# Picks between the maxima, norms transposed inside the up-embedding product, half of the row comparison on GpSimd, keys in two row halves

## The reference

```python
# attention: 16 heads of 16; keys and values from a 64-wide context, causal
qp = layernorm(x) @ Wq.T ; k, v = split(ctx @ Wkv_expand.T)
x = x + tanh(g_xattn) * (softmax(causal(q k^T / 4)) v) @ Wout.T
# experts: 2048, 8 heads, 45 keys for each of two halves of the query
h = silu(layernorm(x) @ W_up.T + b_up) @ W_down.T + b_down
sx, ix = top_k(q0 keys0, 8); sy, iy = top_k(q1 keys1, 8)
sc, pk = top_k(all 64 sums sx + sy, 8); indices = chosen ix * 45 + iy
z = silu((h . down_embed[indices]) * softmax(sc))
x = x + tanh(g_ffn) * sum over (head, k) of z * up_embed[indices]
```

## Time and profile before

| | us |
|---|---|
| median of 3 runs | 1230.05 (1229.36 to 1233.81) |
| profiled execution, its own time | 1228.0 |
| its span | 1226.3 |
| mean granted TensorE clock | 0.983 |

### The profile page before, as it was taken

One profiled execution on the slowest core, in us unless ns is written; L12 is line 12 of the kernel. 1 busy time (PEld: TensorE's weight loads), 2 busy tenths in 40 slices (PEclk: granted clock), 3 DMA queues, 4 the chain that ended last, 5 costly groups with the idle time before them and its releaser, 6 DMA issues. The chain is left out here.

```text
span 1226.3 us, 47601 instructions
## 1 busy us (share of the span) xinstructions
PE 1151.3 (94%) x19004; PEld 1029.6 (84%) x19004; DVE 1071.6 (87%) x4298; ACT 702.8 (57%) x2474; POOL 330.4 (27%) x149
## 2 busy tenths in 40 slices
PE   6778999999999999999999999999999999999957
PEld 4567888888888888888888888889888888988856
DVE  3359999999999999999999999999999999998983
ACT  4565555566655656665555666656566665656310
POOL 4022333212333331223333122333312233331210
PEclk9988999999999999999999999999999999999979
DMA  8015556445645654465565446556544655654454
GB/s 217 13 71 144 106 127 150 122 116 135 147 106 130 150 134 118 121 151 115 118 150 133 123 118 150 118 114 150 135 117 121 150 117 117 149 140 106 130 134 72
DMA packets 304948, 154.52 MB, mean 126 GB/s; under 512 B 282736, under 2 KB 295896, under 8 KB 296536
## 3 DMA queue, kind: packets, MB, share of 16 engines
q1 hardware_dynamic: 304727, 151.47, 51.2%
HBM read 79.62 MB, written 4.72 MB: 69 GB/s over the span
## 5 line engine op out<-in xcount | busy, mean ns | idle before, releaser
L354 POOL TENSOR_TENSOR rstd<-veps,minus_half 128x1 f32<-128x1 f32 x32 | 67.9, 2123 | 718.0 <-DVE veps L805 718.0
L1131 PE MATMUL bank<-ue,coef 128*128 128x256 f32 x1024 | 227.7, 381 | 0.7 <-ACT coef L413 0.7
L1131 PEld LDWEIGHTS bank<-ue,coef 128*128 128x128 f32 x1024 | 193.0, 191 | 25.9 <-ACT coef L413 0.8
L910 PEld LDWEIGHTS bank<-z,hot_rT 128*128 128x128 bf16 x2048 | 155.8, 96 | 42.5 <-issue 29.0
L910 PE MATMUL bank<-z,hot_rT 128*128 128x32 bf16 x2048 | 165.1, 177 | 18.0 <-DVE picked L618 12.6
L453 ACT ACTIVATE P<-bank,smax 128x64 f32<-128x64 f32 x512 | 151.8, 348 | 46.4 <-DVE smax L646 46.2
L927 PE MATMUL bank<-uc,hot_r 128*128 128x32 bf16 x6144 | 161.3, 176 | 13.1 <-issue 12.8
L927 PEld LDWEIGHTS bank<-uc,hot_r 128*128 128x128 bf16 x6144 | 158.1, 96 | 14.9 <-issue 14.2
L910 PE MATMUL bank<-zl,hot_rT 128*128 128x32 bf16 x2048 | 163.9, 177 | 3.6 <-issue 3.6
L910 PE MATMUL bank<-zll,hot_rT 128*128 128x32 bf16 x2048 | 163.9, 177 | 0.2 <-issue 0.2
L910 PEld LDWEIGHTS bank<-zl,hot_rT 128*128 128x128 bf16 x2048 | 156.6, 96 | 3.8 <-issue 3.7
(11 more groups left out here) (142 smaller groups left out, 2301.1 us busy)
## 6 DMA issues: line engine op xcount, KB each, us to landing
hot_rT<-expert_rows SPq DMA_DIRECT2D x64, 1024.0 KB, 6.5
xt<-in_x SPq DMA_DIRECT2D x32, 128.0 KB, 2.4
out<-x1k SPq DMA_DIRECT2D x32, 128.0 KB, 2.1
ct<-in_ctx SPq DMA_DIRECT2D x32, 64.0 KB, 2.1
ue<-in_L_ffn_up_embed SPq DMA_DIRECT2D x1, 2048.0 KB, 13.0
z<-in_L_ffn_W_up SPq DMA_DIRECT2D x1, 1024.0 KB, 8.3
expert_rows<-r_h SPq DMA_DIRECT2D x64, 8.0 KB, 1.8
hot_r<-hot_rT SPq DMA_TRANSPOSE x64, 7.0
```

The costliest lines, as they stand in the source:

```text
L354: nc.gpsimd.tensor_tensor(rstd[:, :], veps[:, :], minus_half[:, :], ALU.pow).then_inc(S["rstd_ok"], 1)
L910: last = mm(bank[:, 32 * (q - 16 * k):32 * (q - 16 * k) + 32], hot_rT[:, q, :], part.rearrange("r (h q) c -> r h q c", h=2)[:, :, q, :], s ...
L1131: last = mm(bG0[:, 0:DM], coef[:, c, :, :].rearrange("r h q -> r (h q)"), ue[:, c, :], start=(c == 0), stop=(c == C - 1))
```

## The change

TensorE puts the transposes of the second norm (`normed_T`) and of the next tile's first norm and context (`inputs_T`, before at the head of the next turn) between the twelfth and the thirteenth of the 16 output products. The second key product takes its operands from partitions 64 to 127 and writes another bank; `k_diag` is written by eight ScalarE instructions of half the size. VectorE does picks 0, maximum 0, picks 1, maximum 1, and the sums later. The second half of the comparison (`hot_T(1)`) is done by GpSimd, as the first thing in its turn.

```diff
 # gpsimd, head of the turn
+                if B:
+                    B.wait_dma("rows_in1")
+                    nc.gpsimd.tensor_scalar(hot_rT[:, Q // 2:Q, :], hot_rT[:, Q // 2:Q, :], p_iota[:, 0:1], None, ALU.is_equal).then_inc(S["hotrT1"], 1)
 # scalar
-                    for h in range(4):
-                        last = nc.scalar.activation(k_diag[:, :, :, h, :], bD[:, 256:512].rearrange("p (a b k) -> p a b k", a=2, b=2),
-                                                    ACT.Copy, scale=head_of[:, h:h + 1])
+                    for a in range(2):
+                        for h in range(4):
+                            last = nc.scalar.activation(k_diag[:, a, :, h, :], (bD, bT)[a][:, 384:512].rearrange("p (b k) -> p b k", b=2),
+                                                        ACT.Copy, scale=head_of[:, h:h + 1])
 # vector
                 if Ct:
                     gathered(0)
-                    gathered_sum(0)
                 if A and (Ct or not Fw):
                     scores_max(0)
+                if Ct:
+                    gathered(1)
+                if A and (Ct or not Fw):
                     scores_max(1)
                 if Ct:
-                    gathered(1)
+                    gathered_sum(0)
+                    gathered(2)
                     gathered_sum(1)
-                    gathered(2)
                     gathered(3)
 ...
                 if B:
                     hot_T(0)
-                    hot_T(1)
 # tensor: new inputs_T(T, ctx_side) and normed_T() hold the transposes that stood inline
+                def inputs_T(T, ctx_side):
+                    T.wait("xn_ok")
+                    T.wait_dma_side(f"ctx_in{ctx_side}")
+                    if B:
+                        B.wait("sm_ok")
 ...
                     for m in range(2):
-                        mm(bD[:, 256 + 128 * m:384 + 128 * m], WkvT[0:CTX, 128 * m:128 * m + 128], ctxT[0:CTX, :, 0, :], start=True, stop=True)
+                        rows = slice(CTX * m, CTX * m + CTX)
+                        mm((bD, bT)[m][:, 384:512], WkvT[rows, 128 * m:128 * m + 128], ctxT[rows, :, 0, :], start=True, stop=True)
 ...
                     for c in range(C):
+                        if c == 3 * C // 4:
+                            if A:
+                                normed_T()
+                            if L:
+                                inputs_T(L, 1 - side)
                         last = mm(bG0[:, 0:DM], coef[:, c, :, :].rearrange("r h q -> r (h q)"), ue[:, c, :], start=(c == 0), stop=(c == C - 1))
```

More of the change, by code:

```diff
@@ L981, in similarity, with normed_T @@
                     mm(bP[s][:, 0:RH * NK], hT[:, :], simW[:, s, :], start=True, stop=True).then_inc(S[f"sim_pe{s}"], 1)
+                def inputs_T(T, ctx_side):
[3 more added lines that the diff above has]
+                        B.wait("sm_ok")
+                    for k in range(2):
+                        nc.tensor.transpose(bT[:, 128 * k:128 * k + 128], xn1[:, 128 * k:128 * k + 128], ident[:, :])
+                    nc.tensor.transpose(bT[:, 256:384], ct[:, ctx_side, :, :].rearrange("p b d -> p (b d)"), ident[:, :]).then_inc(S["xT_pe"], 1)
+                def normed_T():
+                    A.wait("xn2_ok")
+                    if not Fw:
+                        pe.wait_ge(S["wT_act"], 5)
+                    for k in range(2):
+                        last = nc.tensor.transpose(bG1[:, 128 * k:128 * k + 128], xn[:, 128 * k:128 * k + 128], ident[:, :])
+                    last.then_inc(S["x2T_pe"], 1)
                 def probs_T(n):
@@ L994, in probs_T @@
                     last.then_inc(S[f"pt_pe{n}"], 1)
[L996 to L1003, removed]
+                if A and not Fw:
+                    inputs_T(A, side)
                 if Fw and Ct:
@@ L1130, in turn @@
                     for c in range(C):
+                        if c == 3 * C // 4:
[3 more added lines that the diff above has]
+                                inputs_T(L, 1 - side)
                         last = mm(bG0[:, 0:DM], coef[:, c, :, :].rearrange("r h q -> r (h q)"), ue[:, c, :], start=(c == 0), stop=(c == C - 1))
                     last.then_inc(S["out_pe"], 1)
[L1133 to L1139, removed]
+                if not Ct:
+                    normed_T()
+                    if L:
+                        inputs_T(L, 1 - side)
             pe.wait_ge(S["ident_ok"], 1)
```

## The result

The changed kernel takes 1504.94 us (median of 4 runs, 1499.94 to 1509.12); the kernel before took 1231.93 beside it (4 runs, 1229.36 to 1234.13). The ratio is 1.222, with an interval of 1.219 to 1.225. The prediction of 1227 was wrong, and its range, which ended at 1356, did not reach there. The mechanism was its rival A; the stall that A prices at 4.1 us was 8.6.

A forecast was written before the change was run, and what follows sets the result against it. TensorE and a chain through ScalarE and VectorE together were taken to set the 35.49 us turn. The terms gave 31 x -0.1 = -3 us on 1228.0, 1225; plus 2 for the median, 1227, range 1206 to 1356.

The forecast's parts named there:

- rival A: GpSimd's comparison takes the port between two `uc`; scatter waits, +4.1 us a turn, 1354 us (bounds 1335 and 1450); chance 0.28.
- the half comparison on GpSimd: One comparison of 4096 columns moved from VectorE to GpSimd: 4.1 us there (3.5 to 7.2), VectorE saves 1.24.
- The landing at 477.0: Rows land at about 477.0, in the middle of the `uc` instructions, as the fourth gather comes some 0.8 us earlier.
- the two undisturbed `hot_T`: On VectorE, the `hot_T` pair lost nothing (1.2 us start to start) though GpSimd waited; taken as evidence that VectorE keeps its place.
- my forecast's order: GpSimd's comparison runs behind the `uc`, 479.5 to 483.6; `sums` waits up to 2.0 us; costs nothing to 0.1 a turn.
- one wait of 0.42: Wait ahead of the second `up_silu` on VectorE, taken to absorb the 0.6 us by which zl, zll come late.
- Keys: Key products in two row halves: 0 to -0.32 us off the chain; eight `k_diag` on ScalarE +0.58, lower bound 0.
- Norms: Transposes inside the output product: `up(0)` follows it without a gap, -0.31 us a turn.
- Picks: Picks between the maxima on VectorE: ends the fourth gather's 0.34 us stall; picks 3 lose a wait, -0.1 us to `zp`.
- the slack of 0.2: Slack between TensorE and the chain: `uc` was there 0.2 us ahead of scatter, so +0.17 leaves the turn unchanged.
- rival B: Smaller `k_diag` cost at most half each, maxima and picks overlap better: -0.5 us a turn, 1214 us; chance 0.24.
- the row of the bias copies: ScalarE's 128-column bias copies start 0.25 us apart; taken as nearest row, so eight `k_diag` cost 2.0 us against 1.42.

The follow-up runs named there:

- the probe: Kernel before with extra GpSimd instructions of several forms in the set-up, where VectorE leaves it alone; two kernels, 1265.97 and 1256.40 us, one run each.
- e3_pool_after_uc: Changed kernel with GpSimd's comparison also waiting for the last `uc`; 1434.19 us, ratio 1.167 to the kernel before.
- e1_no_pool: Changed kernel with the second half of the comparison back on VectorE; 1242.14 us, ratio 1.011 to the kernel before.
- e_best: Kernel before with norms inside the output product and a picks order keeping distance between sums and waiting picks; no time given, order added nothing to norms alone.

## Why the prediction was wrong

**The step that failed** is the half comparison on GpSimd, twice over. Its size first: 4.1 us, at most 7.2, against 10.8 measured. I took 0.97 ns a column from one-input rows, an affine select and a cast; the probe shows the affine select at 0.92 still, and the tensor-scalar at 2.6. The nearest row by the number of inputs was not the nearest by form, and my upper bound, a difference of two tiles, was no bound. The range stopped short even of that: A reached 1450 by my own bounds, and I took in only its middle, 1354. The Trainium skill (GPSIMD Engine Reference, Engine selection) calls one-input work roughly line-rate, which I had turned into 3.4 us; for this form the run shows 10.6, and the measurement decides.

Then its place. I had it behind `uc`, where it would cost 0 to 0.1. In 26 of 32 tiles it ran between two `uc`, rival A, to which I gave 0.28. The landing at 477.0, 1.8 us behind the first `uc`, was nearly right (2.5 in the median, still 1.0 ahead of the last), and I let the two undisturbed `hot_T` outweigh it. The rule of the Trainium skill (SBUF — State Buffer, Who interferes with whom), that a two-input VectorE instruction and a reading GpSimd one exclude each other and the first to start has its way, holds here in the main: 8.6 us in `uc` or 6.4 in `sums`. It says "for the whole instruction", and there the measurement differs: GpSimd's takes 10.6 to 11.2, the hold is 8.6. A with the measured hold gives 31 x (8.6 - 0.1) = 264, or 1494; measured 1505. So A's mechanism was right and its term mis-sized. That the sum comes so near is in part luck: there were 26 such turns and not 31, and the other parts of the change cost 0.43 a turn where I had taken -0.1.

**Nor was my forecast's order harmless.** `e3_pool_after_uc` forces it and takes 1434: I had weighed a stall in `sums` against one wait of 0.42 only. (The 2.0 less 1.24 there are 0.76; I went on with 0.6. Beside a stall of 6.7 that is nothing.) VectorE's whole idle time in the steady part of before was 48 of 700 us, 2.4 a turn, which its 87% over the span does not tell; TensorE's wait for `sm_in` (4.0 in most turns of `e3_pool_after_uc`) I had not priced at all.

**The terms without GpSimd** gave -0.1 a turn, and `e1_no_pool` shows 36.11 instead of 35.6, with 13.2 us in all, or 0.43 a turn. Its time line, ScalarE and VectorE:

```profile
501.05 2.16 ACT L510 ACTIVATE k_diag<-bank,head_of 128x128 f32<-128x128 f32 x8
503.04 1.20 ACT L422 ACTIVATE P<-bank,bup_sb 128x128 f32<-128x128 f32 x4
504.93 0.69 DVE L653 SCALAR_TENSOR_TENSOR up_act<-up_act,P 128x512 f32<-128x512 f32 x1 [0.61 <-ACT up_act L429]
508.04 0.69 DVE L647 TENSOR_REDUCE smax<-bank 128x8 f32<-128x512 f32 x1
508.76 0.42 DVE L626 TENSOR_REDUCE zs<-picked 128x16 f32<-128x256 f32 x1
509.31 0.86 DVE L619 TENSOR_TENSOR picked<-bank,hot_c 64x256 f32<-64x256 f32 x2
...
512.42 0.23 DVE L733 TENSOR_TENSOR zp<-zs,p_sm 128x64 f32<-128x64 f32 x1
```

- Keys: from the first `k_diag` to the start of what follows, 503.04 - 501.05 = 1.99 us, where I had taken 2.0 against 1.42. Right.
- Norms: -0.31 taken, -0.32 measured alone by the times (9.8 us in 31 turns). Right; in the changed kernel `up(0)` follows the output product without a gap (514.79, where that is modelled to end at 514.95):

```profile
513.06 1.89 PE L1153 MATMUL bank<-ue,coef 128*128 128x256 f32 x8
514.79 1.95 PE L945 MATMUL bank<-xn2T,WupT 128*128 128x128 f32 x16
```

- Picks: from `up_silu` to `zp` it was 473.37 - 466.24 = 7.13; here it is 512.42 - 504.93 = 7.49. I had taken -0.1 and measured +0.36. Two things make this up. Picks 2 and 3 each wait for the sum directly ahead of them and begin 0.13 behind its end (508.76 + 0.42, then 509.31), where in the kernel before picks 2 begin 0.03 behind a sum that they don't wait for: 2 x 0.10. And the two maxima, which ran one behind the other, took 469.39 - 468.18 = 1.21; apart they take 0.72 each (508.76 - 508.04): 0.23 more. The picks give back some 0.08, as their wait is gone. `e_best`, which parts the maxima but keeps the distance, has 7.37, just the 0.24 above 7.13. I had called it the same instructions in another order; the order has a price. The lines of before:

```profile
468.18 1.29 DVE L646 TENSOR_REDUCE smax<-bank 128x8 f32<-128x512 f32 x2
469.39 0.85 DVE L618 TENSOR_TENSOR picked<-bank,hot_c 64x256 f32<-64x256 f32 x2
```

The sum is now -0.31 + 0.58 + 0.36 = +0.63, less the slack of 0.2: +0.43 a turn, 13 us, which is what `e1_no_pool` shows by its time (by the median turns it is 0.5). My chance for rival B, faster by this chain, was too high with 0.24: it needed the `k_diag` to cost no more than half each, against the row of the bias copies.

The three small parts and the large one do not add up: ratios of 1.011 and 1.152 against 1.222. The order of the picks, which alone costs 1.4%, moved the landing of the rows ahead of the last `uc` (the 3.44 and 4.63 us above).

How much of the 273 us the lower clock took for itself stays open, since its stretches grew with the stalls. As an estimate from the rows: TensorE's idle time grew by 222 us ahead of the scatter and by 19 ahead of `sm_in`, and `e1_no_pool` has 13 for the other parts; of the 273 that leaves some 19 for the clock and all else, if these terms don't overlap.

## What to carry to other kernels

Before moving an instruction to GpSimd, time that very form in a probe; a row of another form says little, even with the same number of inputs. Then ask which two-input VectorE instruction will be in flight when it becomes ready, and who waits for that one; the busy share of GpSimd (27% before) says nothing of it. And where a chain on VectorE sets the turn, the order of its instructions is a term of the sum: here an instruction directly behind the one it waits for began 0.10 us later than one that waits for nothing there, and two reductions lost 0.23 by being parted.

## What the runs showed that I had not expected

- A GpSimd instruction gets its way at the boundary of two back-to-back VectorE instructions, though the next `uc` is ready to run: GpSimd's starts at 489.49, the fourth `uc` runs on to its end, and the fifth is the one that stands still (9.27 us).
- VectorE is held for less than the whole instruction: in the second turn `sums` ends at 545.60, so it started by 544.91, where GpSimd's instruction ends at 546.78, 1.9 later. The held `uc` likewise ends 1.2 us ahead of GpSimd's instruction, in each of the 26 cases.
- A memset on GpSimd, which reads nothing, held up a VectorE cast of uint32 to f32 from 189 to 1236 ns while `sums` and `uc` stayed untouched. The two `sm_in` behind the cast rose too, from 221 to 1079 ns; they read two tiles, but as they end with the cast, what they show is most likely its delay.
- A stall of 0.93 us at the fourth gather went with a stretch at 1.2 GHz in each turn; one of 0.34 there did not, nor did one of 0.89 at `dense`.
